# Weighted neighbour rows summed and turned on TensorE: identity products against transpose mode, in a four-layer graph-attention kernel

## The reference

```python
h = jnp.maximum(_layernorm(x, axis=-1), 0.0)
x = x + _L0_gnn_ref(h, ...)   # additive scores, batch norm, elu
x = x + _L1_gnn_ref(h, ...)   # 4 heads, then a second attention over the heads' output
x = x + _L2_gnn_ref(h, ...)   # dot-product scores, leaky relu
x = x + _L3_gnn_ref(h, ...)   # additive scores, relu
# every layer:
attn = softmax(where(adj > 0, scores, very_negative))
out  = einsum('bnm,bmo->bno', attn, rows)
```

## Time and profile before

| | before |
|---|---|
| median of 3 runs | 1629.47 us (1628.49 to 1634.34) |
| the profiled execution: its own time | 1637.15 us |
| its span, first to last instruction | 1635.2 us |
| mean granted TensorE clock | 0.860 |
| busy share of the span: DVE, PE, POOL, PEld, ACT | 76%, 67%, 62%, 49%, 49% |

### The profile page before, as it was taken

The page is one execution under the profiler, slowest core; times in us unless marked ns, Lnnn a source line. Parts: engine busy times, 40 slices in busy tenths (PEclk is TensorE's granted clock), DMA queues, the critical chain, the costliest instruction groups (busy, mean ns, idle before and its releaser), DMA issues.

```text
span 1635.2 us, 19221 instructions
## 1 busy us (share of the span) xinstructions
PE 1089.8 (67%) x5895; PEld 807.0 (49%) x5895; DVE 1239.9 (76%) x1592; ACT 796.1 (49%) x2666; POOL 1017.0 (62%) x965
## 2 busy tenths in 40 slices
PE   0137556742999998699999956567426657766482
PEld 0024322322788887699988722222125557762130
DVE  7889577985999999987878069989758775656461
ACT  2035435663565655356655624566754464463221
POOL 2223488415989878487776668887458643327881
PEclk9999786976999999799999987777767778897797
DMA  9941576402222321011110054422035422227666
GB/s 344 218 180 58 162 200 174 137 32 97 69 62 77 102 61 38 15 33 40 34 46 14 14 167 135 141 84 84 26 125 171 136 72 72 66 86 228 183 192 157
DMA packets 101583, 177.04 MB, mean 108 GB/s; under 512 B 47488, under 2 KB 56224, under 8 KB 99424
## 3 DMA queue, kind: packets, MB, share of 16 engines
q0 software_dynamic: 31472, 102.93, 21.8%
q1 hardware_dynamic: 67280, 72.13, 14.0%
q10 hardware_dynamic: 2720, 0.68, 0.2%
HBM read 145.78 MB, written 34.10 MB: 110 GB/s over the span
## 4 chain that ended last, share of the span: by engine, by line
DVE 35%; PE 24%; POOL 16%; issue 11%; ACT 8%; DMA 3%; another core or an unknown queue 0%; ACTq 0%; DVEq 0%; POOLq 0%; SPq 0%
PE PS L1358 16%; POOL big L693 9%; DVE big L1782 8%; DVE big L1774 7%; ACT big L993 4%; POOL big L720 3%; DVE big L1666 2%; PE PS L1369 2%; DVE big L1602 2%; DVE big L1778 2%; PE PS L1382 2%; PE PS L1414 2%; DVE big L1766 2%; DVE big L1723 1%; DMA big<-in_adj 1%
## 5 line engine op out<-in xcount | busy, mean ns | idle before, releaser
L1358 PE MATMUL PS<-ident,big 128*128 128x128 f32 x3480 | 435.6, 288 | 79.2 <-ACT big L1102 57.0
L1358 PEld LDWEIGHTS PS<-ident,big 128*128 128x128 f32 x3480 | 428.7, 204 | 85.8 <-ACT big L1102 60.9
L993 ACT ACTIVATE big<-big 128x64 f32<-128x64 f32 x1496 | 371.7, 338 | 155.1 <-DVE big L1739 97.5
L720 POOL TENSOR_TENSOR big<-big 128x512 f32<-128x512 f32 x373 | 378.2, 1044 | 104.1 <-DVE big L1739 79.9
L1782 DVE TENSOR_REDUCE big<-big 128x32 f32<-128x2048 f32 (+4 forms) x126 | 297.7, 2362 | 4.4
L1339 PE MATMUL PS<-big,ident 128*128 128x512 f32 x348 | 189.7, 704 | 119.3 <-ACT big L993 61.8
L1774 DVE TENSOR_TENSOR big<-big,PS 128x2048 f32<-128x2048 f32 (+4 forms) x84 | 198.5, 2363 | 48.2 <-PE PS L1369 45.5
L693 POOL DMA_INDIRECT big<-tab,SI x142 | 182.4, 1285 | 78.9 <-issue 41.3
L1339 PEld LDWEIGHTS PS<-big,ident 128*128 128x128 f32 x348 | 76.1, 227 | 222.9 <-issue 209.6
L693 POOL DMA_INDIRECT big<-h_rows,SI x142 | 137.4, 968 | 51.2 <-issue 27.8
L1355 PE MATMUL PS<-big,ident 128*128 128x512 f32 x174 | 111.5, 807 | 66.0 <-POOL big L720 55.6
(11 more groups left out here) (181 smaller groups left out, 1655.0 us busy)
## 6 DMA issues: line engine op xcount, KB each, us to landing
big<-in_adj SPq DMA_DIRECT2D x16, 1024.0 KB, 5.7
tab<-big SPq DMA_DIRECT2D x64, 132.0 KB
big<-tab SPq DMA_DIRECT2D x32, 264.0 KB
h_rows<-big SPq DMA_DIRECT2D x32, 256.0 KB
big<-h_rows SPq DMA_DIRECT2D x32, 256.0 KB
big<-in_x SPq DMA_DIRECT2D x16, 256.0 KB, 5.2
big<-xs SPq DMA_DIRECT2D x4, 1024.0 KB, 9.1
h_table<-big SPq DMA_DIRECT2D x16, 256.0 KB
```

Source lines behind the costliest of these rows:

```text
L720: ins = pool.tensor_tensor(bd(wbuf[:, i % NWB, j, :]), bd(rows[:, k + j, :]), over_d(S[:, h, k + j, :], B), ALU.mult)
L993: ins = act.activation(to, row, ACT.Copy, scale=S[:, h, k + j, b:b + 1])
L1358: mm = pe.matmul(to[:, q * P:(q + 1) * P], wbuf[:, i % NWB, k, q * P:(q + 1) * P], ident[:, :], start=(first and q == 0), stop=(last and q ...
```

## The change

The products of units 1 and 3 in `add_up` are issued in TensorE's transpose mode. Operands, destination, the order of the instructions on every engine, the flags that start and end the accumulation, and all waits are the same. The second attention of layer 1 (L1355) and the layers 0 and 3 of the reference (L1346) keep their identity products.

```diff
@@ -1356,7 +1356,8 @@
                                 else:
                                     for q in range(4):
                                         mm = pe.matmul(to[:, q * P:(q + 1) * P], wbuf[:, i % NWB, k, q * P:(q + 1) * P],
-                                                       ident[:, :], start=(first and q == 0), stop=(last and q == 3))
+                                                       ident[:, :], start=(first and q == 0), stop=(last and q == 3),
+                                                       is_transpose=True)
                             mm.then_inc(chunk_summed, 1)
```

## The result

| | before | after |
|---|---|---|
| median | 1631.49 us (4 runs) | 1558.63 us (4 runs, 1557.03 to 1559.02) |
| ratio, 95% interval | | 0.9552, 0.953 to 0.9574 |
| the profiled execution: own time, span | 1637.15, 1635.2 us | 1559.02, 1557.2 us |
| mean granted TensorE clock | 0.860 | 0.841 |

A forecast was written before the change was run, and what follows sets the result against it. DVE was taken to bound unit 1's first half, PE its second, and a PE-ACT loop much of unit 3. Gains 1 + 30 + 3 + 27 - 2 = 59, less 5 for waits, 54: 1576 us from 1629.47, range 1556 to 1662.

The forecast's parts named there:

- What bounds the kernel: DVE bounds unit 1's first half, PE its second; in unit 3 PE's sum lies on a loop through ACT.
- One pass for two: Sums of units 1 and 3: 1740 passes for 3480, a slot falling from 0.892 to 0.446 us.
- Unit 1: Gains of 1 us in the first half, 30 in tiles 8 to 13, about 3 in the last two tiles.
- the three quarters of the ceiling: Unit 1, tiles 8 to 13: 30 us gained, where POOL's ceiling is 41 and DVE's 42.
- the last two tiles: End of unit 1, where the chain PE, ACT, POOL, PE runs without cover: about 3 us more gained.
- Unit 3: Gains of 3 us in tiles 0 to 4, 4 in tiles 5 and 6, 20 in tiles 7 to 15: 27 of 38.8.
- DVE's room of 4.6: Unit 3, tiles 5 and 6: DVE busy 35.4 of 40 us, so at most 4.6 gained; 4 taken.
- the term for the clock: Unit 3: in thin tiles L1445 and the turns run partly at 0.215 us instead of 0.110; 2 us taken off.
- The 5 us for waits not seen: Whole forecast: some 5 us taken off the summed gain of 59 for waits not visible in the rows.
- Rival 1: Turns don't hold the clock up, so PE falls to 1.2 GHz in the sums: 1715 us, or near 1645; chance 0.28.
- Rival 2: The next bound (POOL, DVE, ACT) takes the gain: faster but less, near 1608 us; chance 0.12.
- rival 3: An accumulating block in transpose mode still is two passes, so nothing changes: 1629 us; chance 0.05.

The follow-up runs named there:

- late_tiles: Transpose mode only in unit 1's sums of tiles 8 to 15, on the kernel before: 1591.21 us against 1630.48.
- unit3_only: Transpose mode only in the sums of unit 3, on the kernel before: 1592.17 us against 1630.0.
- early_tiles: Transpose mode only in unit 1's sums of tiles 0 to 7, on the kernel before: 1627.83 us against 1630.48.
- experiments 4 and 5: 4: DVE's unit 1 score reductions halved, kernel before 1603.68 us, changed kernel 1527.03. 5: changed kernel, ACT weighing more of POOL's slots in unit 1, 1547.51.
- unit1_only: Transpose mode only in the sums of unit 1, on the kernel before: 1591.87 us against 1630.0.
- experiment 1: Kernel before, with 100 turns or 50 ordinary products put where PE waits for the first x: 1631.24 and 1629.93 us against 1630.0.
- experiment 6: Changed kernel, with 14 products or 28 turns ahead of the wait for L1102 in tiles 7 to 13 of unit 3: 1551.95 and 1556.71 us.

## Why the prediction was right or wrong

*What bounds the kernel.* Right for PE: it was the bound in the second half of unit 1 (late_tiles) and on the loop of unit 3 (unit3_only), and covered in the first half (early_tiles). Incomplete for DVE: I took its 98% as its own load, but part of it was waiting for POOL (experiments 4 and 5).

*One pass for two.* Right: 1740 passes, 0.11 us each at full clock, so 0.446 us a slot.

*Unit 1.* Forecast 1 + 30 + 3, measured 38.1. The first half gave nothing that can be told from zero. Tiles 8 to 13, from the start of their first sum to the start of tile 14's, took 214.0 us and take 181.7 (181.3 in late_tiles, 185.0 in unit1_only): 29 to 33 us, so the three quarters of the ceiling were right. The thought behind them, that POOL and DVE would hand the lead to each other at a loss, was not tested; both ran at 90% and 98% at once, and part of DVE's 98% was waiting for POOL. The term that was too small is the last two tiles: from the start of tile 14's first sum to the last product they took 42.9 us and take 35.5 (37.1 and 37.2 in the other two runs), 6 to 7 us where I took 3.

*Unit 3.* Forecast 27 - 2, measured 37.8 alone and 33.2 on top of unit 1. By the starts of the sums in unit1_only (whose unit 3 is the old code) and in the changed kernel: tiles 0 to 4 took 58.3 and take 52.9 us, 5.4 (I took 3); tiles 5 and 6 37.35 and 29.8, 7.6 (I took 4, and held DVE's room of 4.6 for a limit); from tile 7's to tile 15's start 123.8 and 103.5, 20.3 (I took 20). Two terms were mis-sized. DVE's load in a stretch between two sums was no limit, because DVE works ahead of the sums: between the starts of tile 5's and tile 7's it was busy for 33.8 of 38 us in unit1_only and for 29.1 of 30 in the changed kernel, where it had reached 96% in the stretch before. And the term for the clock had the wrong sign. The removed passes were not all at full clock: the sum of tile 6 fell from 8.87 to 4.90 us, 3.97 us for 28 passes, where full clock would make it 3.1. The sums of tiles 7 to 14 together fell from 63.6 to 36.6 us, 27 us for 208 passes that full clock prices at 23.2; the steps kept 20.3 of it.

*The 5 us for waits not seen* were not there. Together about 18 of the 19 us that the forecast fell short are these 5, 8 in unit 3 (the clock's 2 among them) and 5 in unit 1. All of them were cautious terms, so they added up instead of cancelling, and the measured time came close to the end of the range. That end was itself loosely worked out: 1 + 41 + 3 + 38.8 are 84 us, which less the 7 for clock and waits is 1553, not 1556.

*The profiled execution.* I wrote that none of its 7.7 us above the median sits in the stages of the change. That was wrong: its unit 3 is 4 to 7 us longer than in three other runs of the same code. The forecast was taken from the median, so nothing came of it.

*The rivals.* Rival 1, with a chance of 0.28, is refuted by the blocks of experiment 1 and by the granted clock of 0.96 in the second half of unit 1. The row that spoke against it, the rise at 1216, was the better guide. Rival 2 did not come, and rival 3 is excluded by the count of passes.

## What to carry to other kernels

An accumulation of float32 blocks through a product with identity, where the result is wanted turned, costs half the passes in transpose mode. What it is worth is read stage by stage: all of it where PE alternates with another engine, up to the next engine's load where PE is the full one, nothing where it isn't. And an engine that is busy for 98% may be waiting: compare the length of its small operations with the same ones elsewhere before calling it a bound.

## What was not expected of the hardware

- Turns brought the clock up by themselves: 9 passes in the first 2 us, 21 from the fifth us on, through a block of 12.77 us; and from 0.50 to 1.00 of granted clock within the 52 turns of one sum.
- DVE operations with both inputs in SBUF were at times held until POOL's run of products ended, up to 11.78 us against some 0.3 to 0.6. A faster PE can make such a run longer: L1729 took 9.9 us in all in 415 to 890 before and 19.9 after, nearly all of it this one operation, beside which POOL no longer waited for PE.
- The length of the idle time alone doesn't tell the level. In the changed kernel the sums of tiles 11 and 12 of unit 3 both stand behind 3.19 us of idle time and the same four groups of PE work, and one took 2.40 us and the other 4.53. In experiment 6 the sums of tiles 9 and 10 started at 1.2 GHz behind 28 passes and then 2.0 us of idle time (4.9 and 4.5 us), while in unit 1 a group behind 2.11 us of idle time had run at full clock.
